# Filter stage of a graph kernel: inputs made one turn ahead, four steps of one node tile summed in PSUM, four row buffers

## The reference

```python
def ssp(x):
    return jax.nn.softplus(x) - LOG2
h1 = h @ aw_W + aw_b
C = 0.5 * (jnp.cos(edge_weight * (PI / CUTOFF)) + 1.0)
Wf = ssp(ssp(edge_attr @ m1_W + m1_b) @ m2_W + m2_b)
Wf = Wf * C[:, None]
msg = h1[src] * Wf
agg = jax.ops.segment_sum(msg, dst, num_segments=n_nodes)
out = ssp(agg @ o1_W + o1_b) @ o2_W + o2_b
```

## Time and profile before

| | |
|---|---|
| timed runs, median of 3 | 6121.58 us (6119.18 to 6132.07) |
| profiled execution, span | 6128.0 us |
| busy in it: PE, DVE, ACT, POOL | 66%, 51%, 32%, 58% |
| filter stage | 4324 to 5265 us |
| `filters` matmuls, L2527 | 403.9 us, 387 ns each |
| sums, L2545 | 210.8 us, 391 ns each |
| `hidden` matmuls, L2517 | 215.0 us, 614 ns each |
| gathers, L2473 | 513.5 us, 1211 ns each, idle before 410.6 |
| additions, L2627, in 4338 to 5265 us | 179.1 us, 422 ns each |

### The profile page before, as it was taken

One profiled execution on the slowest core, in us unless ns is written; L12 is line 12 of the kernel. 1 busy time (PEld: TensorE's weight loads), 2 busy tenths in 40 slices (PEclk: granted clock), 3 DMA queues, 4 the chain that ended last, 5 costly groups with the idle time before them and its releaser, 6 DMA issues. The chain is left out here.

```text
span 6128.0 us, 77751 instructions
## 1 busy us (share of the span) xinstructions
PE 4062.0 (66%) x17164; PEld 2958.9 (48%) x17165; DVE 3143.4 (51%) x7175; ACT 1987.0 (32%) x4687; POOL 3556.1 (58%) x2851
## 2 busy tenths in 40 slices
PE   5599922596777769677677444445688888745553
PEld 5488811353555555355556333333455555533332
DVE  5577636522555542355554344445477777533334
ACT  0122200000665541266563122220477777400000
POOL 0244411277777725677773788865555555478884
PEclk9999966798887879788787655557799999866555
DMA  0000002234665534566552233333234343243332
GB/s 7 24 10 10 10 27 61 77 77 94 172 168 154 158 89 92 135 171 166 153 156 61 62 84 83 84 79 89 71 102 103 103 104 103 79 101 84 84 84 73
DMA packets 511546, 558.56 MB, mean 91 GB/s; under 512 B 302820, under 2 KB 394959, under 8 KB 511005
## 3 DMA queue, kind: packets, MB, share of 16 engines
q0 software_dynamic: 349600, 362.07, 24.5%
q1 hardware_dynamic: 158408, 187.29, 10.7%
q10 hardware_dynamic: 3250, 6.40, 0.4%
HBM read 460.45 MB, written 92.22 MB: 90 GB/s over the span
## 5 line engine op out<-in xcount | busy, mean ns | idle before, releaser
L1259 POOL DMA_INDIRECT sum_gx_sb<-scratch_xw,keep_k_row_step_sb x1272 | 1602.7, 1260 | 469.9 <-issue 351.3
L1372 PE MATMUL sum_a_ps<-sum_gx_sb,sum_sel_sb 125*125 125x258 f32 (+1 forms) x4320 | 1214.4, 445 | 539.5 <-ACT sum_gx_sb L1308 218.9
L1372 PEld LDWEIGHTS sum_a_ps<-sum_gx_sb,sum_sel_sb 125*125 125x125 f32 x4320 | 936.1, 242 | 732.2 <-issue 514.1
L1308 ACT ACTIVATE sum_gx_sb<-sum_gx_sb,sum_wt_sb 125x129 f32<-125x129 f32 x3312 | 981.8, 388 | 561.5 <-DVE sum_wt_sb L1501 527.2
L2473 POOL DMA_INDIRECT filter_gx_sb<-scratch_h,keep_k_src_step_sb x424 | 513.5, 1211 | 410.6 <-DVEq L2620 299.0
L1168 POOL DMA_INDIRECT scratch_grouped<-keep_k_value_sb,keep_k_place_sb x400 | 481.7, 1204 | 272.6 <-issue 137.1
L2917 POOL DMA_INDIRECT source_gx_sb<-scratch_h,source_grouped_sb x424 | 527.5, 1244 | 140.4 <-issue 117.5
L2929 PE MATMUL source_s_ps<-source_gx_sb,source_sel_sb 125*125 125x257 f32 x848 | 370.0, 612 | 310.8 <-DMA source_gx_sb<-scratch_h,source_grouped_sb 310.8
L2929 PEld LDWEIGHTS source_s_ps<-source_gx_sb,source_sel_sb 125*125 125x125 f32 x848 | 246.3, 304 | 434.5 <-issue 172.1
L2527 PE MATMUL filter_ps<-filter_m_sb,filter_h_sb 128*125 128x256 f32 x1728 | 403.9, 387 | 15.6 <-DVE filter_f_sb L2592 15.3
L2527 PEld LDWEIGHTS filter_ps<-filter_m_sb,filter_h_sb 128*125 128x125 f32 x1728 | 318.2, 189 | 141.9 <-issue 98.2
(11 more groups left out here) (513 smaller groups left out, 6861.5 us busy)
## 6 DMA issues: line engine op xcount, KB each, us to landing
scratch_hots<-sum_cuts_sb SPq DMA_DIRECT2D x108, 244.1 KB
filter_sel_sb<-scratch_hots SPq DMA_DIRECT2D x106, 244.1 KB
sum_gx_sb<-scratch_xw,keep_k_row_step_sb POOLq DMA_INDIRECT x1272
scratch_xw<-gate_xsb_sb SPq DMA_DIRECT2D x50, 253.9 KB
scratch_xw<-attend_xsb_sb SPq DMA_DIRECT2D x25, 507.8 KB
filter_ea_sb<-in_ea_t SPq DMA_DIRECT2D x436, 24.4 KB
filter_gx_sb<-scratch_h,keep_k_src_step_sb POOLq DMA_INDIRECT x424
source_gx_sb<-scratch_h,source_grouped_sb POOLq DMA_INDIRECT x424
```

The source lines that it names most:

```text
L1259: nc.gpsimd.indirect_dma_start(out=gx[:, q, j, :], out_offset=None, in_=table, in_offset=bass.IndirectOffsetOnAxis(ap=keep["row_step"][:, ...
L1308: last = nc.scalar.activation(here, here, ACT.Copy, scale=wt[q][:, h, j:j + 1])
L1372: last = mm(psa[b][0:P, half, 0:BF], sel[:, 0, p, j, :], gx[:, q, at, half * BF:(half + 1) * BF], **flags)
```

## The change

- **Order.** VectorE's step for quad n is now f2(n+2), h1(n+3), the two product instructions of n+1, and last the addition of n. TensorE's is hidden(n+4), sums(n), filters(n+3). ScalarE takes the logs of f2(n+1) and of hidden(n+3) together. `ms` has two buffers. The two extra drains and the semaphore `used` are gone; `ms_made` tells GpSimd as well.
- **Sums.** If `part` of a quad is below 25, TensorE accumulates its four steps in the first place of `ps3` and VectorE adds once; else both do as before. Each engine chooses by two `If` blocks. `quad_tiles` loads four quads' numbers at once into registers, on TensorE and on VectorE. `node_tiles` is only called for a mixed quad.
- **Buffers.** `gx` has four buffers, each with a semaphore, and GpSimd gathers quad n when the products of n-4 are made. Its wait for the weights is gone.
- **Loops.** One loop for all engines (`laps`): a lap is four quads; lap -1 is the prologue, 25 laps are the hardware loop, the last six quads are written out. Guards leave out work for quads that don't exist. `ea_free` is given before `agg` is cleared.

The core of the diff (in `load`, `hidden`, `filters`, `make_h1` and `make_f2` only the counts are rewritten for laps):

```diff
+def quad_tiles(nc, keep, first, count, engine):
+
+    _, values = nc.values_load_multi_w_load_instructions(
+        keep["part"][:].rearrange("o s p -> o (s p)")[:, bass.ds(first, count)], engines=(engine,), min_val=0, max_val=NT,
+        skip_runtime_bounds_check_because="parts are made on chip as tile numbers below NT, or NT")
+    return values
...
-    gx = mem.sb("gx", [P, 2, HF, D])
+    LAP = 4
+    QUADS = STEPS // HF
+    LOOPS = (QUADS - 6) // LAP
+    gx = mem.sb("gx", [P, LAP, HF, D])
...
-    f2, lg2 = ([mem.sb(f"{n}{q}", [P, HF, D]) for q in range(2)] for n in ("f2", "lg2"))
-    ms = mem.sb("ms", [P, HF, D])
+    f2, lg2, ms = ([mem.sb(f"{n}{q}", [P, HF, D]) for q in range(2)] for n in ("f2", "lg2", "ms"))
...
+    def laps(engine, lap):
+        lap(-1, LAP)
+        with engine.Fori(0, LOOPS) as i:
+            lap(i, LAP)
+        for i in range(LOOPS, -(-QUADS // LAP)):
+            lap(i, min(LAP, QUADS - i * LAP))
...
-            pool.wait_ge(landed, 16 * 4)
             for step in range(STEPS):
-                j, q = step % HF, step // HF % 2
-                if j == 0:
-                    pool.wait_ge(used, step // HF + 1)
+                j, n = step % HF, step // HF
+                if j == 0 and n >= LAP:
+                    pool.wait_ge(ms_made, n - LAP + 1)
                 nc.gpsimd.indirect_dma_start(
-                    out=gx[:, q, j, :], out_offset=None, in_=dr["h2"], in_offset=bass.IndirectOffsetOnAxis(
-                        ap=keep["src_step"][:, step:step + 1], axis=0)).then_inc(x_in[q], 16)
+                    out=gx[:, n % LAP, j, :], out_offset=None, in_=dr["h2"], in_offset=bass.IndirectOffsetOnAxis(
+                        ap=keep["src_step"][:, step:step + 1], axis=0)).then_inc(x_in[n % LAP], 16)
...
+            def lap(i, count):
+                for r in range(count):
+                    load(i, r + 5)
+                    load_hots(i, r + 2)
 
             sp.wait_ge(ea_free, 1)
-            for n in range(5):
-                if n >= 2:
-                    sp.wait_ge(hid, n - 1)
-                load(n * HF, n % 2)
-                if n < 2:
-                    load_hots(n, n)
-            with sp.Fori(0, TURNS - 1) as i:
-                for q in range(2):
-                    sp.wait_ge(hid, 2 * i + q + 4)
-                    load(i * U2 + (q + 5) * HF, 1 - q)
-                    sp.wait_ge(summed, 2 * i + q + 1)
-                    load_hots(2 * i + q + 2, q)
+            load(-1, 4)
+            laps(sp, lap)
...
+            def sums(i, r, tile):
+                def ready():
+                    pe.wait_ge(ms_made, i * LAP + r + 1)
+                    pe.wait_ge(added, i * LAP + r + 1)
+                    pe.wait_ge(hot_in[r % 2], i * (LAP // 2 * 16) + (r // 2 + 1) * 16)
+
+                with pe.If(tile < NT):
+                    ready()
+                    for j in range(HF):
+                        last = mm(ps3[0:P, 0, :], sel[:, r % 2, j, :], ms[r % 2][:, j, :], start=(j == 0), stop=(j == HF - 1))
+                    last.then_inc(summed, 1)
+                with pe.If(tile > NT - 1):
+                    ready()
+                    for j in range(HF):
+                        last = mm(ps3[0:P, j, :], sel[:, r % 2, j, :], ms[r % 2][:, j, :], start=True, stop=True)
+                    last.then_inc(summed, 1)
+
+            def lap(i, count):
+                if runs(i, 0):
+                    tiles = quad_tiles(nc, keep, i * LAP, count, mybir.EngineType.PE)
+                for r in range(count):
+                    hidden(i, r + 4)
+                    if runs(i, r):
+                        sums(i, r, tiles[r])
+                    filters(i, r + 3)
 
             pe.wait_ge(landed, 16 * 4)
-            hidden(0, 0, 16 * HF)
-            hidden(1, 1, 16 * HF)
-            filters(0, 0)
-            hidden(2, 0, 32 * HF)
-            filters(1, 1)
-            with pe.Fori(0, TURNS) as i:
-                for q in range(2):
-                    n = 2 * i + q
-                    hidden(n + 3, 1 - q, (i + 2 + q) * (16 * HF))
-                    filters(n + 2, q)
-                    pe.wait_ge(ms_made, n + 1)
-                    pe.wait_ge(added, n + 1)
-                    pe.wait_ge(hot_in[q], i * 16 + 16)
-                    for j in range(HF):
-                        last = mm(ps3[0:P, j, :], sel[:, q, j, :], ms[:, j, :], start=True, stop=True)
-                    last.then_inc(summed, 1)
+            laps(pe, lap)
...
+            def lap(i, count):
+                for r in range(count):
+                    parts = []
+                    if runs(i, r + 1):
+                        act.wait_ge(f2_made, i * LAP + r + 2)
+                        parts.append(filters[(r + 1) % 2])
+                    if runs(i, r + 3):
+                        act.wait_ge(hid, i * LAP + r + 4)
+                        parts.append(hidden[(r + 3) % 2])
+                    log(parts)
...
+            def products(i, r):
+                if runs(i, r):
+                    dve.wait_ge(log2_made, i * LAP + r + 1)
+                    vec.scalar_tensor_tensor(f2[r % 2][:], f2[r % 2][:], 0.0, lg2[r % 2][:], ALU.max, ALU.add)
+                    dve.drain()
+                    dve.wait_ge(x_in[r % LAP], i * (16 * HF) + (r // LAP + 1) * (16 * HF))
+                    vec.tensor_tensor(ms[r % 2][:], f2[r % 2][:], gx[:, r % LAP], ALU.mult).then_inc(ms_made, 1)
+
+            def add(i, r, tile):
+                def one(to, j):
+                    here = agg[:, bass.ds(to, 1), 0:D].rearrange("p o f -> p (o f)")
+                    last = vec.tensor_tensor(here, ps3[0:P, j, :], here, ALU.add)
+                    dve.drain()
+                    return last
+
+                with dve.If(tile < NT):
+                    dve.wait_ge(summed, i * LAP + r + 1)
+                    one(tile, 0)
+                with dve.If(tile > NT - 1):
+                    dve.wait_ge(summed, i * LAP + r + 1)
+                    tiles = node_tiles(nc, keep, (i * LAP + r) * HF, HF)
+                    for j in range(HF):
+                        one(tiles[j], j)
+                dve.nop().then_inc(added, 1)
+
+            def lap(i, count):
+                for r in range(count):
+                    make_f2(i, r + 2)
+                    make_h1(i, r + 3)
+                    if r == 0 and runs(i, 0):
+                        tiles = quad_tiles(nc, keep, i * LAP, count, mybir.EngineType.DVE)
+                    products(i, r + 1)
+                    if runs(i, r):
+                        add(i, r, tiles[r])
+                    else:
+                        dve.drain()
...
             for q in range(2):
                 vec.memset(ea[:, q], 1.0)
             vec.memset(half[:], 0.5)
+            dve.drain()
+            dve.nop().then_inc(ea_free, 1)
             for t in range(0, NT + 1, 13):
                 vec.memset(agg[:, t:t + 13, 0:D], 0.0)
             dve.drain()
-            for sem in (ea_free, added, used, used):
-                dve.nop().then_inc(sem, 1)
+            dve.nop().then_inc(added, 1)
             dve.wait_ge(landed, 16 * 4)
-            make_h1(0, 0)
-            make_h1(1, 1)
-            make_f2(0, 0)
-            make_h1(2, 0)
-            make_f2(1, 1)
-            with dve.Fori(0, TURNS) as i:
-                for q in range(2):
-                    n = 2 * i + q
-                    dve.wait_ge(log2_made, n + 1)
-                    vec.scalar_tensor_tensor(f2[q][:], f2[q][:], 0.0, lg2[q][:], ALU.max, ALU.add)
-                    tiles = node_tiles(nc, keep, i * U2 + q * HF, HF // 2)
-                    dve.drain()
-                    dve.wait_ge(x_in[q], (i + 1) * (16 * HF))
-                    vec.tensor_tensor(ms[:], f2[q][:], gx[:, q], ALU.mult)
-                    tiles += node_tiles(nc, keep, i * U2 + q * HF + HF // 2, HF // 2)
-                    dve.drain()
-                    dve.nop().then_inc(ms_made, 1)
-                    dve.nop().then_inc(used, 1)
-                    make_h1(n + 3, 1 - q)
-                    make_f2(n + 2, q)
-                    dve.wait_ge(summed, n + 1)
-                    for j in range(HF):
-                        here = agg[:, bass.ds(tiles[j], 1), 0:D].rearrange("p o f -> p (o f)")
-                        vec.tensor_tensor(here, ps3[0:P, j, :], here, ALU.add)
-                        dve.drain()
-                    dve.nop().then_inc(added, 1)
+            laps(dve, lap)
 
 
 def nodes_filter(nc, mem, dr, keep, agg):
```

109 lines of the change are left out of this document (55 added, 54 removed).

## The result

| | before | after |
|---|---|---|
| timed runs, median | 6120.38 us (6113.10 to 6132.07, 4 runs) | 5983.13 us (5975.22 to 5990.86, 4 runs) |
| ratio | | 0.9775, interval 0.9760 to 0.9789 |
| profiled execution, span | 6128.0 | 5981.2 |
| filter stage: weights issued, last addition ended | 4328.8 to 5264.5, 935.7 | 4323.7 to 5122.1, 798.4 |
| of it, up to the first sums | 45.8 | 38.2 |

The stage alone gives 137.3 in the two traces; that the two agree to a tenth is chance, since each median is known to some us. The other 9.5 us between the spans lie in code that both kernels share, 5.1 ahead of the stage and 4.4 behind it, and such parts differ as much between the traces of the experiments.

What follows compares the result with a forecast made beforehand. A ring through TensorE, VectorE and ScalarE, not one full engine, was taken to bound the filter stage. Steady steps -94.6, start -7.0 and end -13.1 made -114.7 us, from 6121.58 to 6007; range 5995 to 6062, some 83%.

Steps and rivals of the forecast that it cites:

- ring of 7.66: Second ring, ScalarE's log, VectorE's h1, f2 behind it, next log: 7.66 us a quad, said to go with the new order.
- fast half: Of the old kernel's alternating quads on TensorE, the one lasting 7.45 us without idle time; the other lasted 9.40.
- S begins at 1.87, F at 3.79, the next H at 7.45: TensorE's new step: start times of sums, filters and next hidden matmuls, its own work unchanged at 7.45 us a quad.
- no overhead at all: Low end of the forecast: branches, loads and mixed quads cost nothing, 6000 us, less 5 for the measurement.
- I take 0.2 for each of 26 laps: TensorE's load of `part`, once in four quads, mostly hidden behind queued filter passes: 5.2 us in all, bounds 0 and 31.
- Start: Filter stage's start: `ea_free` before the two memsets issues SyncE's first load 6.7 us earlier; first sums 7.0 us earlier.
- End: Filter stage's last quads: no work for quads that don't exist, end 6.9 before the even count of S(105), saving 13.1 us.
- worth nothing beyond that slack: VectorE's one addition instead of four: its step is 5.5 us, idle 2 us, so the saving itself gains nothing.
- The part is needed by the new pace: GpSimd's four row buffers: worth 0, but two would leave gathers one step, 7.45 minus 6.06 and the landing.
- slack about 1.5 in its own round: SyncE's loads of edge tiles and hot rows: 5.9 us of work a step, slack about 1.5.
- Rivals 1 to 5: Exposed load 6033, 12%; 7.66 ring stays 6029, 8%; exposed branches 6091, 10%; old pace 6101 to 6115, 3%; slower 6206, 4%.
- Rival 3: TensorE's branches exposed, 0.5 us a quad, and the loads: 105 x 0.5 + 31 = 84, 6091 us; chance 10%.

Runs made afterwards that it cites:

- no_if: Changed kernel without branches or TensorE's load of `part`, every quad accumulated and added once, mixed quads' result left wrong: 5981.27 us, one execution.
- pe_loads: Changed kernel with TensorE's load of `part` made for each quad behind the hidden matmuls, not once in four quads: 5987.61 us, one execution.
- f_first: Changed kernel with filters ahead of sums on TensorE, and VectorE's f2, h1 and products one step earlier: 6126.65 us, 1.0006 of before.
- f_first_b: Filters ahead of sums again, but SyncE loads hot rows of n+1, then edge tiles of n+6, in a step: 5996.35 us, 0.9792 of before.

## Why the prediction was wrong, point by point

**What bounded the kernel before** was read rightly, as a ring and not a full engine: the old order with one addition keeps the ring of 7.66 to a hundredth. What was missed is a wait inside the fast half.

**The failed step is "S begins at 1.87, F at 3.79, the next H at 7.45" and the sum 105 x 7.45 built on it.** I took the fast half of the earlier trace rows, which "has no idle time", for TensorE's own work. It held 0.20 of waiting for the products, hidden under a modelled end and visible only at the weight loads. The floor is 7.25; 105 x 0.20 = 21 us; the other terms that were off, 6.4 of overheads and 0.7 of the start more, 5.5 of the end less, nearly cancel, and make it 22.6. No rival was faster than the forecast, and the low end, "no overhead at all", took 7.45 as given, so it could not hold the time.

**Overheads.** "I take 0.2 for each of 26 laps" and "0.1, 1.6 us" for mixed quads: 6.8 forecast, 0.4 measured (four steps of 7.35). The load took 333 ns for 784, and no_if and pe_loads show no price at either end. f2 was 0.7 late behind a mixed quad, as worked out, and that did stay hidden. So the steady part is 105 x 7.25 + 0.4 = 761.7 and gave 883.7 - 761.7 = 122.0 where 94.6 was forecast. It is counted for 105 even steps, as in the forecast; that the last ones are shorter is in the end's term.

**Start**: 7.0 forecast, 7.7 measured, of which `ea_free` is 5.2 and not 6.7.

**End**: 13.1 forecast, 7.6 measured. The last addition ended 1.4 before the even count of S(105), not 6.9. The trace of the last quads, after:

```profile
5113.84 1.23 DVE L2636 SCALAR_TENSOR_TENSOR filter_f_sb<-filter_f_sb,filter_lg_sb 125x1024 f32<-125x1024 f32 x1 [0.75 <-issue]
5115.14 1.23 DVE L2639 TENSOR_TENSOR filter_ms_sb<-filter_f_sb,filter_gx_sb 125x1024 f32<-125x1024 f32 x1
...
5117.97 3.56 PE L2566 MATMUL filter_ps<-filter_ms_sb,filter_sel_sb 125*125 125x256 f32 x8 [0.95 <-issue]
5121.68 0.43 DVE L2644 TENSOR_TENSOR keep_agg_sb<-filter_ps,keep_agg_sb 125x256 f32 x1 [4.09 <-PE filter_ps L2566]
```

Products of 105 began at 5113.84 and not 2.6 us earlier, when their log was ready (5111.20), because the four additions of mixed quad 103 stood ahead of them. The last sums took 3.56 instead of 1.99: TensorE had idled for 5.0 and 0.95 before the last two sums, and the granted clock was 0.50, the level of 1.2 GHz, from 5111.0 to 5121.2. Without mixed quads (no_if) the same stretch, S(100) to the last addition, is 29.6 for 35.0. The forecast had used the steady durations for an engine that idles. Together: 122.0 + 7.7 + 7.6 = 137.3 for 94.6 + 7.0 + 13.1 = 114.7.

**Accumulation** was to be "worth nothing beyond that slack": wrong by 21 us (17.6 in the traces). VectorE's step was put at 5.5 with one addition and so near 7.1 with four; against a floor of 7.25 there is no room for the jump. At the forecast's 7.45 the error would have been small; the mis-sized floor made it matter.

**Four row buffers**: worth 0, right. "The part is needed by the new pace" is wrong. Rows for quad n may start at the products of n-2 and are wanted two steps less one instruction later, 13 us, not one step.

**SyncE** ("slack about 1.5 in its own round") was right here, but only because the sums stand second in TensorE's step. f_first and f_first_b show that their place is worth some 130 us through that queue (6126.65 for 5996.35). It belonged among the rivals.

**Rivals 1 to 5** did not come about: no idle before H in fourth quads, no wait for h1, none before S; the ring of 7.66 needs the old order; VectorE's jumps never stopped it, with eleven instruction packets in the whole stage. Rival 3's sum counts the forecast's 5.2 for loads twice (it should be 6086), which changed nothing. By the Trainium skill ("Runtime: NRT & Kernel Launch", Instruction fetch mechanics) a taken branch forces a fetch when its target lies outside the current two-page window. The trace agrees that VectorE's loop stays inside: eleven packets in all, for at least a jump in each of 106 quads.

## What to carry to other kernels

To find what a pipelined matmul group costs by itself, look at the weight loads' idle and at a group whose inputs are surely there, and not only at a row without idle time: a release that comes as the last pass runs out is invisible in the matmul rows. Before a group is moved on one engine, list what an in-order DMA queue waits for on its behalf, since the loads queued behind that wait move with it. An addition or branch that is "hidden" has a price again as soon as the floor it hides under moves down, so slacks should be checked against the lowest floor and not the forecast one.
